# Two quantizers of a gated cross-attention block: the extrema over all partitions by one GpSimd operation instead of by two matmuls

## The reference

```python
def _affine_quantize(x):
    amin, amax = (jnp.min(x), jnp.max(x))
    scale = jnp.maximum((amax - amin) / 255.0, 1e-08)
    zp = jnp.clip(jnp.round(-amin / scale) + QMIN, QMIN, QMAX)
    q = jnp.clip(jnp.round(x / scale) + zp, QMIN, QMAX)
def _qlinear(x, W, b):
    xq, sx, zx = _affine_quantize(x)
    wq, sw = _sym_quantize(W)
    return jnp.einsum('bsh,oh->bso', xq - zx, wq) * (sx * sw) + b
h = gelu(_qlinear(x, W1, b1)); out = _qlinear(h, W2, b2)
x = x + tanh(g_ffn[0]) * out
```

## Time and profile before

| | us |
|---|---|
| median of 3 runs (lowest, highest) | 1523.78 (1521.7, 1525.93) |
| the profiled execution's own time | 1523.75 |
| its span | 1522.0 |
| busy: PE, DVE, ACT, POOL | 1393.4, 1246.8, 898.2, 917.3 |

### The profile page before, as it was taken

The page is one execution under the profiler, slowest core; times in us unless marked ns, Lnnn a source line. Parts: engine busy times, 40 slices in busy tenths (PEclk is TensorE's granted clock), DMA queues, the critical chain, the costliest instruction groups (busy, mean ns, idle before and its releaser), DMA issues. The chain is left out here.

```text
span 1522.0 us, 34257 instructions
## 1 busy us (share of the span) xinstructions
PE 1393.4 (92%) x14575; PEld 577.0 (38%) x14598; DVE 1246.8 (82%) x1281; ACT 898.2 (59%) x1050; POOL 917.3 (60%) x697
## 2 busy tenths in 40 slices
PE   6999999779999999999999999999989869874997
PEld 2444444223333333333333333333334334432343
DVE  5877677688888888888888888888738889998876
ACT  4332333147767676767676767676764878763453
POOL 7421111078888888888888888888865579900100
PEclk9999999999999999999999999999999979996999
DMA  9765564852153213321332133210028526545885
GB/s 305 213 215 173 190 214 141 209 145 64 33 143 85 71 33 88 85 69 36 88 85 64 40 88 85 62 42 19 23 88 286 193 111 270 228 165 194 302 305 194
DMA packets 126925, 207.11 MB, mean 136 GB/s; under 512 B 11956, under 2 KB 65204, under 8 KB 125248
## 3 DMA queue, kind: packets, MB, share of 16 engines
q1 hardware_dynamic: 117504, 186.68, 39.6%
q10 hardware_dynamic: 5856, 9.44, 1.9%
q0 software_dynamic: 3424, 8.95, 1.8%
HBM read 124.29 MB, written 72.35 MB: 129 GB/s over the span
## 5 line engine op out<-in xcount | busy, mean ns | idle before, releaser
L763 POOL TENSOR_TENSOR x<-x 128x512 f32<-128x512 f32 x512 | 672.5, 1326 | 135.7 <-ACT x L817 129.1
L852 DVE TENSOR_REDUCE row_max<-ring 128x1 f32<-128x1024 f32 x512 | 610.2, 1215 | 98.2 <-PE ring L662 96.1
L817 ACT ACTIVATE x<-ring 128x1024 f32<-128x1024 f32 x512 | 513.9, 1024 | 235.5 <-PE ring L724 234.6
L686 PE MATMUL o_acc<-x,v 128*32 128x512 f32 x2048 | 264.2, 592 | 3.2 <-ACT x L817 2.3
L724 PE MATMUL ring<-ffn_w_int 128*32 128x512 f16 x2560 | 193.9, 380 | 6.0 <-DVE row_max L852 6.0
L662 PE MATMUL ring<-ffn_w_int 128*32 128x512 f16 x2560 | 193.7, 379 | 6.1 <-DVE row_max L852 6.1
L695 PE MATMUL sum_acc<-x,ones 128*32 128x512 f32 x1024 | 132.1, 592 | 1.6 <-POOL x L763 1.6
L662 PE MATMUL ring<-x 128*32 128x512 f16 x1536 | 119.3, 392 | 15.1 <-DVE row_max L852 11.1
L1466 PE MATMUL down<-ffn_w_int,hq 128*128 128x512 bf16 x502 | 114.6, 386 | 18.1 <-ACT hq L1452 17.7
L1254 PE MATMUL hid<-xqT,ffn_w_int 128*128 128x512 bf16 x499 | 117.4, 385 | 10.4 <-ACT xqT L1284 8.7
L724 PEld LDWEIGHTS ring<-ffn_w_int 128*32 128x32 f16 x2560 | 62.9, 96 | 152.5 <-DVE row_max L852 79.4
(11 more groups left out here) (208 smaller groups left out, 2036.0 us busy)
## 6 DMA issues: line engine op xcount, KB each, us to landing
scratch_G<-gelu SPq DMA_DIRECT2D x56, 512.0 KB, 2.7
g_in<-scratch_G SPq DMA_DIRECT2D x28, 1024.0 KB, 6.2
x<-in_ctxT SPq DMA_DIRECT2D x8, 1024.0 KB, 6.9
x<-in_x SPq DMA_DIRECT2D x8, 1024.0 KB, 8.6
v<-scratch_V SPq DMA_DIRECT2D x16, 512.0 KB, 8.4
scratch_V<-x SPq DMA_DIRECT2D x28, 256.0 KB, 3.1
out<-x POOLq DMA_DIRECT2D x7, 1024.0 KB, 7.5
ffn_w_int<-scratch_QH SPq DMA_DIRECT2D x20, 256.0 KB, 4.0
```

The source lines that it names most:

```text
L686: last = nc.tensor.matmul(oacc[h * DK:(h + 1) * DK], v[buf][:, kt, h * DK:(h + 1) * DK], prob[:, s % 2, h, part], tile_position=(0, h * DK ...
L763: nc.gpsimd.tensor_tensor(pair[:, s % 2, h], prob[:, s % 2, h, 0], prob[:, s % 2, h, 1], ALU.add).then_inc(pair_done, 1)
L817: nc.scalar.activation(prob[:, s % 2, h], ring[slot][:], ACT.Exp, scale=SM_SCALE).then_inc(exp_done, 1)
L852: nc.vector.tensor_reduce(mraw[:, i:i + 1], ring[slot][:], AX.XY, ALU.max).then_inc(max_done, 1)
```

## The change

In both quantizers the turning matmul, the column maximum, the diagonal, the second matmul and the copy go, with their semaphores and their two small tiles. In their place GpSimd runs one `partition_all_reduce` from `top` to `all`. In `stage_up` it stands ahead of GpSimd's wait for `coef_ready`, in `stage_down` at the start of its block, ahead of the output DMAs.

```diff
     def __init__(self, nc, ctx, name):
-        self.diag = ctx.enter_context(nc.sbuf_tensor(f"{name}_top_diagonal", [2, 2], F32))
-        self.column = ctx.enter_context(nc.sbuf_tensor(f"{name}_top_column", [2, 1], F32))
...
-    def across(self, nc, pe, k, turned, spread):
-        pe.wait_ge(self.top_ready, 1)
-        nc.tensor.transpose(turned, self.top[:], k.id32[:]).then_inc(self.top_turned, 1)
-        pe.wait_ge(self.diag_ready, 1)
-        nc.tensor.matmul(spread, k.ones_rows[:], self.diag[:], start=True, stop=True).then_inc(self.all_ready, 1)
+    def across(self, nc, pool):
+        pool.wait_ge(self.top_ready, 1)
+        nc.gpsimd.partition_all_reduce(self.all[:], self.top[:], P, bass.bass_isa.ReduceOp.max).then_inc(self.all_ready, 1)
...
         nc.vector.tensor_reduce(self.top[:], tops[:].rearrange("p n m -> p m n"), AX.X, ALU.max).then_inc(self.top_ready, 1)
-        dve.wait_ge(self.top_turned, 1)
-        chain(nc.vector.tensor_reduce(self.column[:], turned, AX.X, ALU.max))
-        nc.vector.tensor_scalar(self.diag[:], k.id32[0:2, 0:2], self.column[:, 0:1], None, ALU.mult).then_inc(self.diag_ready, 1)
         dve.wait_ge(self.all_ready, 1)
-        chain(nc.vector.tensor_copy(self.all[:], spread))
         top, neg = self.all[:, 0:1], self.all[:, 1:2]
...
# stage_up, block of GpSimd
+            par.across(nc, pool)
             pool.wait_ge(coef_ready, 2)
# stage_down, block of GpSimd
+            par.across(nc, pool)
             for c, n in enumerate(CHUNKS[:-1]):
# both, block of TensorE
-            par.across(nc, pe, k, turned, spread)
```

## The result

The changed kernel takes 1546.55 us (median of 4 runs, 1545.22 to 1547.89) against 1523.84: a ratio of 1.015, 95% interval 1.0138 to 1.0162. The profiled execution took 1546.83 us with a span of 1545.0. I had forecast 1536.4 in a range of 1530 to 1540: the direction was right, the loss was nearly twice as large, 23.0 us of span instead of 12.6.

A forecast was written before the change was run, and what follows sets the result against it. VectorE was taken to bound stage_up, and stage_down's small quantizer chain to be paid in full. 1523.75 + 8.3 (stage_up) + 4.3 (stage_down) = 1536.35 us, 0.8% slower, with a range of 1530 to 1540 us.

The forecast's parts named there:

- What the removed work is worth: Both quantizers: the matmul chain between top reduction and line 1334 is worth at most 1.87 us each, 3.74 in all.
- An all-reduce is preceded by a fetch: Both quantizers: 5.95 us from top reduction to all-reduce, delaying line 1334 by 4.28 us in stage_up, 4.30 in stage_down.
- The return: stage_up, after the all-reduce: GpSimd's second configuration costs 5.95 us, odd tiles start 9.1 us later, tile 1 7.3 later.
- rival A: stage_up: return to ordinary GpSimd code is free, all shifts by 4.3 us, total 1532.35 us; chance 0.16.
- rival B: stage_up: return dearer than the fetch, 8.9 us gives 1539.35 us, 15.4 us about 1546; chance 0.12.
- VectorE 0.5 us back for less contention: stage_up: GpSimd's line 1190 comes later against VectorE's seven tiles, so the first gelu extremum is +6.8 us.
- The debt at tile 12: stage_up: ScalarE waits 1.8 us for GpSimd's line 1190, VectorE's next run comes 1.5 us later still, stage +8.3 us.
- Stage down: stage_down: first clip +4.3 us behind the all-reduce; loads and output DMAs add nothing.
- The next launch: Launch start, line 205: a 5.95 us exchange makes GpSimd's identities ready at 11.9 us, ScalarE needs them at 12.57; costs nothing.
- C: stage_up: fetch quicker without DMAs, 3 us, stage about +2.5 us, total 1530.55 us; chance 0.09.
- D: Both quantizers: code stays on GpSimd or fetch under 1.5 us, gain up to 1.45 us each, 1520.85 us; chance 0.03.
- The clock and the output DMAs: TensorE's clock returns at the same work, only later; stage_down's GpSimd output DMAs move with VectorE and cost nothing.

The follow-up runs named there:

- e6: Changed kernel plus unread all-reduces ending GpSimd's stage_attend and stage_up blocks, and an ordinary GpSimd operation behind the last all-reduce: 1527.55 us, ratio 1.0017.
- e3: Changed kernel, but SP holds back all its first stage_down loads until the all-reduce is done: 1542.99 us, ratio 1.0132.
- e11: Changed kernel, but SP issues one 1 MB stage_down load at once and holds the others until the all-reduce is done: 1544.74 us, one run.
- e4: Kernel before, both quantizers keeping their matmuls, plus one unread all-reduce between two GpSimd output DMAs in stage_down: 1531.44 us, ratio 1.0045.
- e1: Changed kernel with the all-reduce in stage_up alone, stage_down back on the matmuls: 1534.87 us, ratio 1.0066.
- e2: Changed kernel plus one ordinary one-column GpSimd operation behind the stage_down all-reduce: 1542.40 us, ratio 1.0118.
- e8: e6 with ScalarE scaling all eight first tiles and GpSimd's bias of tiles 4 to 7 moved to its list's end: 1522.78 us, ratio 0.9987.
- e7: Kernel before with the all-reduce only in stage_down, an unread one ending GpSimd's stage_up block, and an ordinary operation behind: 1523.09 us, ratio 0.9993.
- e12: e4 with GpSimd's fills of constant rows in stage_project moved behind its first context chunk: 1535.12 us, ratio 1.0069.

## Why the prediction was wrong in size

*What the removed work is worth:* right. At most 1.87 us per place, I said; e6 shows 0.71 against 2.09 us, so 1.4 us net.

*An all-reduce is preceded by a fetch:* right, and in `stage_up` the size as well. From the start of the `top` reduction to the all-reduce are 5.84 us against 5.95; line 1323 came 6.24 us after the reduction against a forecast of 6.4.

*The return:* right in kind. The odd tiles started 7.0 us behind the all-reduce, not within 1 us (rival A) and not after 8.9 (rival B). Tile 1 was handled 13.99 us after `x_top` against 5.81 before, +8.2 for a forecast of +7.3. The return was 7.0 and not 5.95 us, which makes up that 0.9. I gave VectorE 0.5 us back for less contention; it didn't come. Two operations of line 1212 take 1.26 us there as before, and the two of tile 1, now beside GpSimd's line 1184, take 1.01 and 0.88 us instead of 0.47 and 0.72, 0.7 us more. The first gelu extremum was therefore +8.9 (24.61 against 15.74 us behind `x_top`), not +6.8.

*The debt at tile 12:* it exists, but did not move the end. ScalarE waited 0.76 us for line 1190 at 1269.82 and 2.8 us in all, while the whole stage is longer by just the +8.9 of that first extremum. My 8.3 for the stage was close since two errors cancelled.

*Stage down:* a term mis-sized. The fetch took 9.2 us beside SP's loads instead of 5.95, and the first clip is +7.8 (11.60 us behind `h_top` against 3.79), not +4.3. I took the fetch in `stage_attend`, beside 368 GB/s, for an upper bound on traffic, from a single row; e3 and e11 show that traffic of another kind costs 3.5 us more.

*The next launch:* this step failed. I wrote "It hides it with 0.7 us to spare: nothing." The mechanism was as described, but the return at line 205 took 11.6 us where I had put 5.95. It ran beside 344 GB/s, which may be why; no run takes that traffic away. The constants came at 17.3 us. I had also misread when ScalarE needs them: not at 12.57, where its table load starts (12.58 in the changed kernel, constants or not), but at 13.87, where the operation behind it stands in the kernel before:

```profile
13.87 0.20 ACT L368 ACTIVATE root_table_spare<-eps 128x1 f32<-128x1 f32 x1
```

So a return of 5.95 us would have had 2.0 us to spare; one of 11.6 us makes ScalarE 3.5 us late. And I had asked only who waits for GpSimd, not who is slowed by GpSimd's fills if they come later: they now lie beside VectorE's normalizing. e4 has this step alone and costs 6.7 us; e1 and e2 take it away.

*Rivals:* A, C and D are out: the return is real, a quiet fetch takes 5.6 us and not 3, and neither all-reduce came without one. (C's odd tiles at +3.2 us also need a return of 3 us; with one of 5.95 they would be at +6.2.) B was nearest in its total of 1539 to 1546, but by 7.0 instead of 8.9 us it had the wrong place. The clock and the output DMAs show no cost: neither of the last two stages is longer by more than its first extremum or clip is late.

In sum: of the 10.4 us that the span of the changed kernel lies above the forecast, 6.9 are the start, 2.9 `stage_down` and 0.6 `stage_up`.

## What to carry to other kernels

Price a GpSimd library operation by the idle time behind its configuration and not by its record, once on the way in and once on the way back, and count the next launch as well. Where it must be used, run it once for nobody while GpSimd is idle, give the first work behind it to another engine, and leave ordinary code on GpSimd before the launch ends, in a stretch where nobody needs it. With all of that the gain over the matmuls was about 0.1% here (e8). A price taken from one row is a point and not a bound: look at what else moved beside it, and where work of one engine moves, look at whom it then lies beside.

## What the runs showed of the hardware

- Between a configuration and its all-reduce GpSimd stood idle for 5.6 to 6.3 us with no DMA beside it, 7.5 with one 1 MB load and 8.6 to 9.2 with all of them. Between an all-reduce and the next ordinary operation it was 6.8 to 7.2 us quiet, 8.2 to 11.2 beside loads (e2, e6, e7, e8), and 9.8 to 11.9 at the start of a launch. A second all-reduce with nothing ordinary in between paid neither (e6).
- The changed kernel's windows count 0 GB/s over the fetch in `stage_up`, and the profile's two instruction queues hold 107 and 34 packets in every run, with or without the new all-reduces. What fills the gap shows in no DMA row of the profile.
- What a launch leaves on GpSimd is still there at the next one: one all-reduce that nobody reads, late in the launch, moved the first `affine_select` of the next from 4.2 to 15.2 us (e4), and in the changed kernel an ordinary operation behind the last all-reduce moved it back to 4.2 (e2).
- GpSimd's memsets of 4096 f16 columns stretch some VectorE operations beside them, `tensor_scalar` and casts: four operations of line 404 from 1.91 to 7.56 us, a cast from 0.43 to 3.15. A `TENSOR_TENSOR` (0.69 us in e12, 2.29 in the kernel before) took no longer beside them.
